# Performer features in a fused four-layer kernel: four heads per product, high and low parts stacked in the rows of the array

## The reference, cut to what matters

```python
def softmax_kernel(x, proj, is_query):          # x: b, 16 heads, 1024, 16; proj: 64 x 16
    norm = x.shape[-1] ** (-0.25)
    ratio = proj.shape[0] ** (-0.5)
    xp = jnp.einsum('bhnd,md->bhnm', x * norm, proj)
    diag = jnp.sum(jnp.square(x), axis=-1, keepdims=True) * 0.5 * (norm * norm)
    if is_query:
        stab = jnp.max(xp, axis=-1, keepdims=True)
    else:
        stab = jnp.max(xp, axis=(-1, -2), keepdims=True)
    return ratio * (jnp.exp(xp - diag - stab) + EPS_K)
...
qp, kp = softmax_kernel(q, proj, True), softmax_kernel(k, proj, False)
k_sum = jnp.sum(kp, axis=2)
denom = jnp.einsum('bhnm,bhm->bhn', qp, k_sum)
ctx = jnp.einsum('bhnm,bhnd->bhmd', kp, v)
out = jnp.einsum('bhnm,bhmd->bhnd', qp, ctx) / denom[..., None]
```

## Time and profile before

| | us |
|---|---|
| Median of 3 runs | 2685.26 |
| The runs | 2656.91, 2685.26, 2687.45 |
| The profiled execution | 2670.26 |
| Its span | 2668.6 |
| PE busy | 2419.6 (91%) |
| DVE busy | 1781.3 (67%) |
| ACT busy | 1275.4 (48%) |
| Mean granted TensorE clock | 0.951 |

### The profile page before, as it was taken

One profiled execution on the slowest core, in us unless ns is written; L12 is line 12 of the kernel. 1 busy time (PEld: TensorE's weight loads), 2 busy tenths in 40 slices (PEclk: granted clock), 3 DMA queues, 4 the chain that ended last, 5 costly groups with the idle time before them and its releaser, 6 DMA issues. The chain is left out here.

```text
span 2668.6 us, 43935 instructions
## 1 busy us (share of the span) xinstructions
PE 2419.6 (91%) x16088; PEld 2223.2 (83%) x16088; DVE 1781.3 (67%) x3348; ACT 1275.4 (48%) x2026; POOL 710.7 (27%) x468
## 2 busy tenths in 40 slices
PE   6988996899889969999999999984999997899999
PEld 6878885888888868898898898873999996799998
DVE  5666565899999966566567556525667764767664
ACT  4444443434443325455456446424666763444443
POOL 1110011444444433023212312303444431211110
PEclk9999997999999989999999999966999999899999
DMA  5000000000000000000000000001000010000000
GB/s 171 0 0 0 0 0 19 1 1 0 0 0 0 1 17 1 17 8 8 16 8 8 16 12 8 12 24 55 17 24 24 16 40 29 14 25 17 23 24 32
DMA packets 42827, 45.68 MB, mean 17 GB/s; under 512 B 2944, under 2 KB 41728, under 8 KB 42496
## 3 DMA queue, kind: packets, MB, share of 16 engines
q1 hardware_dynamic: 42752, 44.68, 5.1%
HBM read 27.90 MB, written 16.78 MB: 17 GB/s over the span
## 5 line engine op out<-in xcount | busy, mean ns | idle before, releaser
L1828 DVE TENSOR_TENSOR m_a_lo<-m_a,m_a_hi 128x512 fp32r<-128x512 f32 x128 | 106.0, 830 | 127.9 <-ACT m_a_hi L1787 127.9
L1783 ACT ACTIVATE d_a<-d_ps_wide,d_b 128x512 f32<-128x512 f32 x128 | 88.3, 690 | 190.5 <-PE d_ps_wide L271 188.5
L1828 DVE TENSOR_TENSOR d_a_lo<-d_a,d_a_hi 128x512 fp32r<-128x512 f32 x128 | 86.7, 689 | 111.7 <-ACT d_a_hi L1787 111.1
L1269 POOL TENSOR_TENSOR p_kf<-p_kf,p_k_shift 128x1024 f32<-128x1024 f32 x64 | 119.4, 1902 | 155.4 <-DVE p_k_shift L1403 155.4
L1746 PE MATMUL m_ps_z<-m_w_hi,m_a_hi 128*128 128x256 f32 x512 | 147.6, 288 | 8.8 <-DVE m_w_lo L1807 8.8
L1783 ACT ACTIVATE m_a<-m_ps_wide,m_b 128x512 f32<-128x512 f32 x128 | 88.0, 687 | 122.2 <-PE m_ps_wide L271 122.1
L1746 PE MATMUL m_ps_z<-m_w_hi,m_a_lo 128*128 128x256 f32 x512 | 145.7, 285 | 0.0
L1746 PE MATMUL m_ps_z<-m_w_lo,m_a_hi 128*128 128x256 f32 x512 | 145.5, 284 | 0.0
L1746 PE MATMUL d_ps_z<-d_w_hi,d_a_lo 128*128 128x256 f32 x512 | 145.4, 284 | 0.0
L1746 PE MATMUL d_ps_z<-d_w_lo,d_a_hi 128*128 128x256 f32 x512 | 145.0, 283 | 0.0
L1746 PE MATMUL d_ps_z<-d_w_hi,d_a_hi 128*128 128x256 f32 x512 | 143.9, 281 | 0.3 <-DVE d_a_lo L1828 0.3
(11 more groups left out here) (348 smaller groups left out, 8613.1 us busy)
## 6 DMA issues: line engine op xcount, KB each, us to landing
residual<-in_x SPq DMA_DIRECT2D x8, 1024.0 KB, 11.8
attn<-p_attn SPq DMA_DIRECT2D x32, 256.0 KB, 2.2
m_attn<-attn SPq DMA_DIRECT2D x16, 512.0 KB, 3.7
out<-residual SPq DMA_DIRECT2D x16, 512.0 KB, 2.9
raw_weights<-in_d_q SPq DMA_DIRECT2D x2, 1024.0 KB, 7.2
d_scale<-in_d_scale SPq DMA_DIRECT2D x2, 1024.0 KB, 5.7
raw_weights<-in_m_w1T SPq DMA_DIRECT2D x1, 1024.0 KB, 4.9
raw_weights<-in_m_w2T SPq DMA_DIRECT2D x1, 1024.0 KB, 6.9
```

The source lines that it names most:

```text
L1269: pool.tensor_tensor(f, f, k_shift[:, i, :].unsqueeze(2).broadcast_to([P, HEADS, M]), ALU.subtract).then_inc(k_shifted, 1)
L1783: act.activation(self.a[f % RING][:, :], self.ps_wide[f % 2][:, :], self.func, bias=self.b1[:, f:f + 1])
L1828: dve.tensor_tensor(self.a2[1][:, f, :], self.a[f % RING][:, :], self.a2[0][:, f, :].bitcast(F32), ALU.subtract).then_inc(self.a_lo, 1)
```

## The change

A stationary tile now holds four heads instead of eight, twice: their high parts in one half of the 128 rows, their low parts in the other. `kqT[0]` has heads 0 to 3 of a chunk (high in rows 0 to 63, low in rows 64 to 127), `kqT[1]` heads 4 to 7 (high in rows 64 to 127, low in rows 0 to 63). The projection is a block-diagonal matrix for four heads, 128 x 256, the same in both halves of the rows. One product with its high part gives high x high and low x high together; a second one with its low part, which is zero in the rows of the low halves, adds high x low. Per tile the 6 matmuls of 512 columns become 8 of 256 columns; those of a pair have the same stationary operand.

ACT writes the high part of a projection in two instructions of 64 partitions instead of one of 128, and DVE the low part in two as well, each from 64 partitions of PSUM to the other 64 partitions of SBUF. The signals stay where they were, behind the last instruction of each group. The preparation, once per run, splits a projection of 256 columns instead of 512 and clears half of each low part. Tiles, order and waits are otherwise unchanged.

```diff
+HH = HC // 2
+HALVES = slice(0, HH * DH), slice(HH * DH, 2 * HH * DH)
...
         for h in range(HC):
-            sync.dma_start(self.proj[h * DH:(h + 1) * DH, h * M:(h + 1) * M], dram["p_projT"]).then_inc(self.loaded, 16)
+            at = h % HH * M
+            sync.dma_start(self.proj[h * DH:(h + 1) * DH, at:at + M], dram["p_projT"]).then_inc(self.loaded, 16)
...
-        proj = pair("p_proj", [P, HC * M])
+        proj_hi = sbuf("p_proj_hi", [P, HH * M], F32R)
+        proj_lo = [sbuf(f"p_proj_lo{s}", [P, HH * M], F32R) for s in range(2)]
...
-                split(dve, part(proj, slice(None)), raw.proj[:, :], step)
+                step.add(dve.tensor_copy(proj_hi[:, :], raw.proj[:, :]))
+                step.wait()
+                for s, rows in enumerate(HALVES):
+                    step.add(dve.memset(proj_lo[s][HALVES[1 - s], :].bitcast(F32), 0.0))
+                    step.add(dve.tensor_tensor(proj_lo[s][rows, :], raw.proj[rows, :], proj_hi[rows, :].bitcast(F32), ALU.subtract))
...
-        kqT = pair("p_kqT", [P, KD, S])
+        kqT = [sbuf(f"p_kqT{s}", [P, KD, S], F32R) for s in range(2)]
...
-                dve.scalar_tensor_tensor(kqT[1][:, c, cols], bank, bias["kq"[k]][:, c:c + 1],
-                                         kqT[0][:, c, cols].bitcast(F32), ALU.add, ALU.subtract).then_inc(kq_lo, 1)
+                for s, rows in enumerate(HALVES):
+                    mm = dve.scalar_tensor_tensor(kqT[s][HALVES[1 - s], c, cols], bank[rows], bias["kq"[k]][rows, c:c + 1],
+                                                  kqT[s][rows, c, cols].bitcast(F32), ALU.add, ALU.subtract)
+                mm.then_inc(kq_lo, 1)
...
-                act.activation(kqT[0][:, c, cols], bank, ACT.Identity, bias=bias["kq"[k]][:, c:c + 1])
+                for s, rows in enumerate(HALVES):
+                    act.activation(kqT[s][rows, c, cols], bank[rows], ACT.Identity, bias=bias["kq"[k]][rows, c:c + 1])
...
                 for c in range(KD):
-                    mm = product(pe, ps_feat[i % 2][:, c * BANK:(c + 1) * BANK],
-                                 part(kqT, slice(None), c, slice(i * P, (i + 1) * P)), part(proj, slice(None)))
+                    for s in range(2):
+                        out = ps_feat[i % 2][:, c * BANK + s * HH * M:c * BANK + (s + 1) * HH * M]
+                        kq = kqT[s][:, c, i * P:(i + 1) * P]
+                        pe.matmul(out, kq, proj_hi[:, :], start=True, stop=False)
+                        mm = pe.matmul(out, kq, proj_lo[s][:, :], start=False, stop=True)
```

More of the change, by code:

```diff
@@ L1087, in __init__ @@
         self.w = raw[:, 0:self.FREE].rearrange("p (n c d) -> p n c d", n=4, c=KD)
-        self.proj = raw[:, self.FREE:self.FREE + HC * M]
+        self.proj = raw[:, self.FREE:self.FREE + HH * M]
         self.qf = [raw[:, self.FREE + s * HEADS * M:self.FREE + (s + 1) * HEADS * M] for s in range(2)]
```

## The result

The changed kernel takes 2762.64 us (median; 2742.37 to 2769.57) where the kernel before, run beside it, takes 2673.61 (2656.91 to 2687.45). The ratio is 1.0321, with a 95% interval of 1.0274 to 1.0368. The forecast of 2701 and its range, 2640 to 2755, were both too low. The profiled execution after took 2742.37, with a span of 2740.7; the 72 us between it and the profile before are what the traces can be asked about.

A forecast was written before the change was run, and what follows sets the result against it. PE was taken as the bound, busy for 2419.6 of 2668.6 us. From 2670.3, 55.8 off and 35 given back made 2649; 52 for two cold tails (at the low clock) made 2701, range 2640 to 2755.

The forecast's parts named there:

- PE's gross, 55.8: Feature product on PE: 128 tiles each save 0.436 us, 55.8 us off as the upper bound of the gain.
- The give-back of the split, 35: Extra ACT and DVE instructions make PE wait in merged stages, front and tails: 9 + 6 + 10 + 10 = 35 us lost.
- The start of the tail: Head of each tail: stabiliser comes 1.0 us later, last squares 0.2 late; 8 x 1.2 = 10 us lost.
- The clock, booked as 52 for cold tails and nothing else: Tails: two of the four with low stretches stay at the low clock, about 26 us each, 52 in all.
- How the clock comes back: F(0) and F(1) in the tail: 5.3 us of dense matmuls raised the clock; 3.4 us after the change may not.
- Rival 1: Tails: the clock behaves as now, or low stretches miss the tails; 2649 us (2635 to 2665), chance 0.23.
- Rival 3: Tails: four or more go cold (stay at the low clock); 2753 us with four, chance 0.16.
- Rival 4: Split on DVE: writing across partitions costs double, 0.75 us more at each of 64 splits; 2689 us, chance 0.08.
- Rival 2: PE keeps all it saves, ACT and DVE on 64 partitions cost half or less; 2614 to 2632 us, chance 0.08.
- D: Theory of the experiments, not the prediction: tail tiles with fewer feature columns can't hold the clock; 18 to 24 us per tail.

The follow-up runs named there:

- the split alone: Kernel before with its ACT and DVE instruction each cut into two of 64 partitions, features as before: 2716.77 us, ratio 1.0187.
- the thinned kernel before: Kernel before with one product of three left out of q's features in the tail (other values than the reference's): 2742.51 us, ratio 1.0276.
- one form with the moved stabiliser: Changed kernel, stabiliser's matmul moved behind q's fourth projection: 2751.51 us with eight products added in the half squares, 2789.94 without; the text doesn't say which is meant.
- cutting the half squares in two: Changed kernel with the features of q's tile 0 put between the two groups of half squares: 2855.86 us, ratio 1.0678.
- the whole-partition kernel: Changed kernel with one ACT and one DVE instruction of 128 partitions per projection (other values than the reference's): 2755.89 us, ratio 1.0337.

## Why the prediction was wrong, step by step

Put in ratios, of about 2670 us: the changed kernel is 3.2% over. Putting the columns back in the tail takes 2.45 of it away (65 us, work added). Writing whole partitions takes another 1.4 (37 us). What is left is -0.6 (17 us), most of it the gain of the merged stages.

- **PE's gross, 55.8: right in price, half of it in place.** The merged stages on whole partitions are 3.1 us shorter where eight tiles of 0.436 make 3.5. The rule of the Trainium skill that the prediction weighed ("TensorE: Matmul & The Clock Gate", Back-to-back issue gap) would have made them longer; the trace's 0.230 and 0.118 held. A warm tail with the thin tiles is 34.8 us at best for 36.4, 1.6 and not 3.5; the prediction had booked such a loss (1.2 a tail).
- **The give-back of the split, 35: right in sum.** With the stabiliser's wait, which the table has in the merged stages, 22 of it were booked there (9 + 6 + 7 x 1.0); it is 7 x 3.8 = 27. About 12 were booked for the tails; 0.9 a tail, 7, is what the split alone shows. The low `mixedT` makes PE wait three times a stage, as forecast, up to 1.5 us. The start of the tail was priced at 1.0 for the stabiliser and has 1.8 - 0.3 = 1.5.
- **The clock, booked as 52 for cold tails and nothing else: the step that failed.** The two cold tails of the profiled execution have tiles of 6.83 us (forecast 6.7 to 6.8) and cost about 55 with the stages behind them (forecast 52). Without them it would have taken 2687, not 2649. Of these 38 us, about 6 lie ahead of the first tail and behind the last, and 8 in the merged stages. Some 24 lie in the tails, and by this estimate they are mostly dips: the prediction's terms give 37.7 - 3.5 + 1.4 = 35.6 a tail, and a thin tail at its best with the split's 0.9 is 35.7, but the six warm tails take 38.7 on average, with 7 to 12 us at the low clock in each. The prediction left the dips as they were, in four tails.
- **How the clock comes back was misread.** The prediction took all of F(0) and F(1), 5.3 us, for what raised it each time. In batch 0 of the kernel before, F(0) starts at 1040.83 and the low stretch of the earlier trace rows ends at 1044.2, with a third of the twelve still to come. After the change F(0) and F(1) at the low clock take 3.6 us, and the clock was back within them or right behind in six tails of eight, and not in two. That two went cold, as forecast, is partly luck: they are batches 2 and 6, and batch 6 has no dip in the kernel before. Cold stretches also start 15 to 21 us into a tail, at a wait for an exponential, which no term of the prediction had.
- **The median lies 20 over the profiled execution**, and so over the range. No trace of the other three was taken, but the mean granted clock of each is on record: 0.918 for the profiled one, 0.915, 0.909 and 0.908 for 2756, 2769 and 2770 us. Twice the missing share of the clock, times the span, is the time at the low clock: the last two have 54 and 60 us more of it than the profiled one and take 26 and 27 us longer. That is what one more cold tail each, with the stage behind it, would make.
- **Rivals.** Rival 1's condition (the clock comes back behind the half squares) held in six tails of eight, and its 2649 still failed, by the dips. Rival 3 gave the right side and nearly the right time (2753 with four cold tails), with 0.16; by the trace it is two cold tails, or three in slower executions, and the dips. Rival 4 is refuted: crossing partitions costs nothing, 750 ns. Rival 2 is refuted by its own test, half durations.

What stays open: which tails go cold. In the thinned kernel before and in one form with the moved stabiliser it is every third batch, and two kernels that differ by the stabiliser's place have none and three. D doesn't say when a thin tail falls or whether it comes back, and the wait for the exponential is not separated from it. Nor is it shown why cutting the half squares in two was so costly.

## What to carry to other kernels

In this kernel, streaming less did not take less time, because the granted clock fell with it. Before thinning the dense part of such a loop, try the thinning alone with the old instructions: one product left out told it here in one run. Then ask which waits the shortened part used to cover. If the clock is lost in a thin part, products that nobody reads can be worth more than they cost (2762.6 to 2695.9 here). And a cut of an instruction along the partitions cost a whole instruction, paid where it stood in an engine's queue ahead of one that was waited for.

## What the runs showed of the hardware

- ScalarE and VectorE take 682 and 750 ns for 64 partitions of 512 columns, and 688 and 751 for 128. For VectorE, reading one half of the partitions and writing the other is free: 750 ns with it and without it.
- In the whole-partition kernel's trace, tails of the same code take 36.5 us with 6.8 at the low clock and, a batch later, 54.2 with 44.6. With a third of the feature columns out of the tail's tiles, a low stretch could last to the projections of the next stage (48 to 75 us); with them in, 17.1 us at most.
- PE at 100% busy in the profile doesn't mean that the clock is held: the stretches of 51.2 us at 0.50 in the whole-partition kernel have no idle time at all. Small matmuls (34 columns, 0.107 us apart warm, 0.205 cold) are busy in the records, and some of the falls lie among them.
- Single waits of 1.7 to 1.8 us in front of thin work stood ahead of many falls. Taking one away moved the falls and didn't end them.
- The last stage with the same instructions ran at the low clock in most kernels (5.92 us a tile in the kernel before), and at 2.4 GHz in one (3.46) with nothing added to the stage.
